# Order of scores steps and transposed steps on TensorE in the first and third stretch of a slot of a fused attention and expert-layer kernel

## The reference

```python
def attn(x):                      # x already normalised once
    xn = layer_norm(x, ln_g, ln_b)
    q, k, v = xn @ wq + bq, xn @ wk + bk, xn @ wv + bv       # 16 heads of 64
    scores = q @ k.T / sqrt(64)
    scores = where(tril(ones, -1), -inf, scores)             # keys before the query are masked
    h = softmax(scores) @ v
    return h @ w0 + b0 + x
def ffn(x):                       # 8 experts of rank 16, top 2 by the first token
    return x + sum_e gate_e * (x @ down_e.T) @ up_e.T
x = x + layernorm(attn(layernorm(x)))
x = x + layernorm(ffn(layernorm(x)))
```

## Time and profile before

| | |
|---|---|
| median of 3 runs | 982.62 us (981.31 to 984.0) |
| the profiled execution | 981.79 us, its span 980.0 us |
| mean granted clock of TensorE | 0.996 of full speed |
| TensorE busy (matmuls) | 946.4 us, 97% |
| GpSimd busy | 702.4 us, 72% |
| VectorE busy | 636.9 us, 65% |
| ScalarE busy | 538.3 us, 55% |

### The profile page before, as it was taken

How to read it: one execution, slowest core, us unless ns; L and a number is a source line. 1 busy time by engine, 2 the same in 40 slices (tenths; PEclk the granted TensorE clock), 3 DMA queues, 4 the chain that set the end, 5 groups by cost and what they waited for, 6 DMA issues and landing times.

```text
span 980.0 us, 20358 instructions
## 1 busy us (share of the span) xinstructions
PE 946.4 (97%) x7646; PEld 596.7 (61%) x7650; DVE 636.9 (65%) x1867; ACT 538.3 (55%) x731; POOL 702.4 (72%) x517
## 2 busy tenths in 40 slices
PE   8899999999999999999999999999999999999895
PEld 4565666666666566666666656666656665665563
DVE  6676566565666857566857667666666576766367
ACT  5355656454545665664555565665546456465443
POOL 7278777666778877777777778886578777776762
PEclk9999999999999999999999999999999999999999
DMA  4000101121001111101002100011100211011110
GB/s 116 23 1 3 23 23 25 23 45 23 3 23 45 23 24 24 24 9 38 23 24 67 23 14 13 24 24 44 24 23 3 66 23 24 23 24 24 24 44 22
DMA packets 61813, 26.94 MB, mean 27 GB/s; under 512 B 39060, under 2 KB 53780, under 8 KB 61716
## 3 DMA queue, kind: packets, MB, share of 16 engines
q1 hardware_dynamic: 61696, 25.64, 11.4%
q10 hardware_dynamic: 20, 0.00, 0.0%
HBM read 22.76 MB, written 2.35 MB: 26 GB/s over the span
## 4 chain that ended last, share of the span: by engine, by line
PE 87%; DVE 5%; issue 3%; POOL 3%; ACT 2%; DMA 0%; POOLq 0%; ACTq 0%; DVEq 0%
PE po L788 24%; PE st L773 21%; PE sc L736 10%; PE st L698 9%; PE st L768 7%; PE st L854 6%; PE sc L798 3%; PE st L713 2%; PE st L714 2%; PE st L715 2%; DVE stats L1234 1%; DVE sc L1263 1%; DVE k_low L1320 1%; PE st L862 1%; ACT ring L1062 0%
## 5 line engine op out<-in xcount | busy, mean ns | idle before, releaser
L536 POOL TENSOR_TENSOR total<-total,ring 128x1024 f32<-128x1024 f32 (+1 forms) x313 | 538.9, 1722 | 238.0 <-PE po L788 198.1
L1263 DVE CUSTOM_DVE_ANT_0 sc<-sc,key_mask 128x512 f32<-128x512 f32 (+1 forms) x496 | 230.4, 522 | 107.5 <-PE sc L736 103.6
L1062 ACT ACTIVATE ring<-st 128x1024 f32<-128x1024 f32 (+1 forms) x256 | 228.5, 918 | 125.6 <-PE st L773 107.0
L1266 DVE TENSOR_REDUCE least<-sc 128x1 f32<-128x512 f32 x268 | 168.3, 671 | 70.2 <-PE sc L736 68.8
L788 PE MATMUL po<-ring,v_sb 128*64 128x512 f32 (+3 forms) x1280 | 210.7, 467 | 0.0
L773 PE MATMUL st<-q_high,k_low 64*128 64x512 f32 (+3 forms) x768 | 176.8, 447 | 0.0
L788 PEld LDWEIGHTS po<-ring,v_sb 128*64 128x64 f32 x1280 | 86.8, 137 | 129.0 <-issue 123.9
L736 PE MATMUL sc<-k_high,q_high 64*128 64x512 f32 (+3 forms) x768 | 134.4, 380 | 9.1 <-DVE least L1263 3.4
L773 PE MATMUL st<-q_low,k_high 64*128 64x512 f32 (+3 forms) x768 | 136.3, 342 | 0.0
L773 PE MATMUL st<-q_high,k_high 64*128 64x512 f32 (+3 forms) x768 | 136.2, 342 | 0.0
L736 PEld LDWEIGHTS sc<-k_high,q_high 64*128 64x128 f32 x768 | 68.5, 185 | 79.3 <-issue 61.6
(11 more groups left out here) (184 smaller groups left out, 1257.1 us busy)
## 6 DMA issues: line engine op xcount, KB each, us to landing
inv_row<-sums_dram SPq DMA_DIRECT2D x62, 256.0 KB, 4.0
x_a<-x SPq DMA_DIRECT2D x4, 512.0 KB, 5.2
sums<-sums_row SPq DMA_DIRECT2D x124, 2.0 KB, 2.1
x_b<-x SPq DMA_DIRECT2D x3, 512.0 KB, 6.0
out<-res_b SPq DMA_DIRECT2D x3, 512.0 KB, 4.9
total<-w_pairs SPq DMA_DIRECT2D x1, 1152.0 KB, 6.7
shift_row<-shift_t SPq DMA_DIRECT2D x62, 4.0 KB
x_a<-x SPq DMA_DIRECT2D x2, 256.0 KB, 3.4
```

The costliest lines, as they stand in the source:

```text
L536: nc.gpsimd.tensor_tensor(so_far, so_far, tile_of(n, s)[:, :, col:col + w], ALU.add).then_inc(s_add, 1)
L1062: nc.scalar.activation(tile_of(n, s)[:, :, 0:w], st[s % 2][:, :, 0:w], ACT.Exp, scale=SCALE).then_inc(s_exp, 1)
L1263: last = nc.vector.tensor_tensor_reduce(bank[:, col:col + w], bank[:, col:col + w], key_mask[:, 0:w], -1.0, 3e38, ALU.add, ALU.min, least[ ...
L1266: last = nc.vector.tensor_reduce(least[:, h, a:a + 1], bank[:, col:col + w], AX.X, ALU.max, negate=True)
```

## The change

In `ORDER`, which holds for slots 1 to 31, the strings of the first and third stretch change. The second scores step of the stretch now stands behind two transposed steps instead of one, and one transposed step instead of two stands between it and the third scores step. Slot 0 has its own strings and stays as it is, as does the second stretch.

```diff
     S_STEPS = [(1, range(3, 6)), (1, range(6, 9)), (2, range(0, 3))]
-    ORDER = ["STSTTS", "STTSTTS", "STSTTS"]
+    ORDER = ["STTSTS", "STTSTTS", "STTSTS"]
```

## The result

| | before | after |
|---|---|---|
| median | 982.58 us (5 runs) | 994.79 us (993.76 to 995.98, 5 runs) |
| ratio | | 1.0121 (95%: 1.0102 to 1.014) |
| the profiled execution | 981.79 us, span 980.0 us | 995.68 us, span 994.0 us |
| granted clock | 0.996 | 0.997 |

What follows compares the result with a forecast made beforehand. TensorE, busy nearly all of the span, was taken to bound the kernel. Third stretch +21.9 us and first stretch -7.8 gave +14.1, so 996.7 us against the 982.62 median (995.9 from the profiled execution); range 990 to 1002.

Steps and rivals of the forecast that it cites:

- The rule and the place: Third stretch: third scores step waits for VectorE's head 0 read of the second, sums for head 1; sums +0.72 a slot.
- The predicted sign that line 798 would wait on TensorE itself: In the changed profile's waits, the matmuls of the sums were to be held themselves; before, only their weight load was.
- The third stretch's size: Sums later by 0.72 us in 24 slots and 0.92 in 5, together +21.9 us.
- step 3: Third stretch: 0.15 from read's end to waiting matmul; third scores step at 3.69, sums at 4.34 instead of 3.62.
- The five held slots: Third stretch, 5 of 29 slots where VectorE's late k_low holds the first transposed step: +0.92 us each.
- The first stretch: Third scores step earlier: -0.22 us in 26 slots, -0.69 in three, 0 in slot 30; together -7.8 us.
- The two conditions meet: First stretch: VectorE's read (3.50) and the first transposed step's exponentials (3.42 to 3.57) limit the third scores step about equally.
- What costs nothing: Whole kernel: no instruction, DMA or queue entry added or removed; other engines keep their orders; no cost from these.
- Rotation hides the reads anyway: Rival: three rotating banks hide the third stretch's reads, only the first stretch's gain stays; 974.8 us, chance 0.03.
- Only S2 waits, the sums don't: Rival, third stretch: only the third scores step waits, the sums' bank is read early enough; 987.3 us, chance 0.04.
- The clock: Rival: granted clock falls once in each of 29 slots, losing 1.7 us each time; 1046 us, chance 0.01.

Runs made afterwards that it cites:

- the kernel without cover: Changed kernel with no transposed step between the second and third scores steps of the third stretch; 1016.62 us against 982.6, ratio 1.0343.
- the three logit waits: Seen with the v projection put in front of the sums in the changed kernel, in the slots with a router logit; 1007.05 us against 981.86, ratio 1.0262.

## Why the prediction was right, point by point

- **The rule and the place.** Right, in each of 29 slots: S1 predicted at 2.31, measured 2.31 in slot 20; S2 3.69, measured 3.71; no wait at S1. The predicted sign that line 798 would wait on TensorE itself did not come: only its weight load waited, 10.8 us instead of 7.2. The experiments that took away, exchanged and removed the cover show it as cause.
- **The third stretch's size.** Predicted 0.72 and 0.92 a slot, measured 0.65 and 0.86; +21.9 against +19.8. The mis-sized term is in step 3, "sums at 4.19 + 0.15": I carried the reaction of a scores step over to the sums, and theirs is 0.06 (638.75 to 638.81). 0.09 x 29 = 2.6 us, less what the later start of S1's read (0.50 and not 0.47 behind S1) gives back: the third stretches are 2.1 us under their forecast; the first ones gained 0.4 us less than forecast and the second ones 0.2 us: 14.1 - 2.1 + 0.4 - 0.2 = 12.2. The lower bound held it ("at the very least nothing"), the value chosen did not.
- **The five held slots.** Right that the loss is larger there, by 0.2.
- **The first stretch.** Predicted -0.22, -0.69 in three, 0 in slot 30; measured about -0.20, -0.68, -0.11. "The two conditions meet" was right, 0.03 apart; that they came so close is luck, for the rows gave T2 a range of 0.15.
- **What costs nothing.** Right: nothing behind the sums took the delay up, the second stretch stayed, and VectorE's five holds by k_low stayed at 5.6 us in all.
- **The rule of the Trainium skill** (Perfetto Trace Analysis, Matmuls), that rotating banks lets reads overlap the next group's matmuls: the trace agrees as far as there are enough matmuls. With three banks and steps that take two, only what stands between two steps overlaps; with 1.88 of matmuls from S1 to S2 all was hidden, with 0.82 TensorE waited until 1.40.
- **The rivals.** "Rotation hides the reads anyway" would have given what the first stretch alone gives, and that kernel measured 975.0, as its sum had it. "Only S2 waits, the sums don't" was nearer the truth than I gave it room: the sums' read costs 0.12, not the 0.29 between 3.69 + 0.36 and 4.34; but then the held S2 passes on 0.08 more than a free one, which neither sum had. The clock stayed: mean 0.997 after, with 29 new gaps of about 0.4 us. By what the Trainium skill (TensorE: Matmul & The Clock Gate, A second HAM failure mode) tells of short idles between groups it could have fallen; the trace of the changed kernel disagrees, and so does that of the kernel without cover, where gaps of 0.95 us in 29 slots brought no fall behind them. The rival was not empty, though: each of the three logit waits of 1.76 us above was followed by one.
- **What I should have drawn from my own sum.** It said that the two edits have opposite signs, -7.8 and +21.9. The half that gains, run alone, beats both kernels.

## What to carry to other kernels

An order written by hand between steps that share few PSUM banks is to be checked step by step: from the start of one step to the start of the next that needs its bank, is there as much TensorE work as lag, read and reaction take? Here the same string helps in one stretch, where the slow masked read (S3) gets the longer cover, and harms in another, where it (S1) loses it; what looks like one pattern has to follow the slow reads and the narrow tiles. Moving work in front of a wait pays only if nothing waits for the result of what was moved back: look for who asks for its bank next. And a wait can cost more than its length, where the clock falls behind it: read the granted clock of what follows.

## What the runs showed of the hardware

- From a VectorE read's end to a held scores matmul it is 0.14 to 0.15 us, to the sums' matmul 0.06. Why the two differ stays open.
- A scores step that has waited passes TensorE on later: the v projection or the free sums start 0.42 to 0.44 behind it, against 0.32 to 0.38 for the sums behind one that has not. Why stays open.
- A masked read of 128 columns isn't a quarter of one of 512: 0.36 against 0.75 for a head, and with 0.5 of lag before and 0.14 behind it a bank was away for 1.0 us, against 1.34 to 1.40.
- Three waits of TensorE of 1.76 us, each between stretches of dense matmuls, were each followed by a fall of the granted clock to 0.5 that cost 1.7 us more. Gaps of 0.4 us (the changed kernel), 0.95 us (no cover) and 1.1 us (the holds by k_low, in every kernel) were not. The longest idle time inside the slots of any of these runs that no fall followed is 1.62 us (T0's exponentials cut in half, slot 31). What decides stays open.
